# Outputs turned by transposes and chosen on DVE, values of four batches in one visit, tables made within the first tile: a perceiver layer on one core

## The reference, cut to what matters

```python
# stage 1: queries (128, 32, 128), context (128, 257, 128), mask (32, 257)
q, k, v = (a.reshape(B, n, 16, 8) for a in (layernorm(x), ctx, ctx))
A = softmax(einsum('blhe,bshe->bhls', q, k) / sqrt(8)) * mask
x = x + einsum('bhls,bshd->blhd', A, v).reshape(B, 32, 128)
# stage 2: x = x + attention(layernorm(x)) with a decay table in the lag of two tokens, and biases bq, bk, bv, bo
# stage 3: x = x + experts(layernorm(x)), with first-layer bias b1
```

## Time and profile before

| | us |
|---|---|
| median of 3 runs | 1048.88 (1048.84 to 1049.33) |
| profiled execution | 1050.45 |
| its span, first to last instruction | 1048.70 |
| first exponential of stage 1 | 23.97 |
| end of stage 1 (last addition to X) | 529.0 |
| busy: PE, DVE, ACT, POOL | 927.9, 840.0, 648.9, 606.9 |

### The profile page before, as it was taken

One profiled execution on the slowest core, in us unless ns is written; L12 is line 12 of the kernel. 1 busy time (PEld: TensorE's weight loads), 2 busy tenths in 40 slices (PEclk: granted clock), 3 DMA queues, 4 the chain that ended last, 5 costly groups with the idle time before them and its releaser, 6 DMA issues. The chain is left out here.

```text
span 1048.7 us, 25999 instructions
## 1 busy us (share of the span) xinstructions
PE 927.9 (88%) x7666; PEld 815.4 (78%) x7666; DVE 840.0 (80%) x2152; ACT 648.9 (62%) x2006; POOL 606.9 (58%) x531
## 2 busy tenths in 40 slices
PE   3959999999999999999948888878899888888983
PEld 2848888888888888888848888778788787878872
DVE  5747787878788787878758887886499999999995
ACT  2626566656666566666536666666477777767674
POOL 4335555655555564556344444443477777877786
PEclk9979999999999999999969998999999999999997
DMA  4021212212221212221400000000000000000000
GB/s 119 25 74 56 58 50 65 55 47 60 55 65 43 65 55 52 56 65 54 142 1 1 0 0 0 0 0 1 1 2 10 5 10 5 10 5 6 9 5 16
DMA packets 48676, 35.34 MB, mean 34 GB/s; under 512 B 3660, under 2 KB 48392, under 8 KB 48648
## 3 DMA queue, kind: packets, MB, share of 16 engines
q1 hardware_dynamic: 48648, 35.00, 12.2%
HBM read 32.88 MB, written 2.10 MB: 33 GB/s over the span
## 5 line engine op out<-in xcount | busy, mean ns | idle before, releaser
L551 ACT ACTIVATE E<-SC,neg_max 128x257 f32<-128x257 f32 x512 | 238.4, 471 | 161.2 <-DVE neg_max L613 161.1
L425 PE MATMUL SC<-Kt,Qbd 128*128 128x257 f32 x1024 | 279.6, 396 | 1.0 <-ACT E L551 0.8
L613 DVE TENSOR_REDUCE neg_max<-SC 128x2 f32<-128x514 f32 x256 | 177.0, 691 | 86.6 <-PE SC L425 75.2
L425 PEld LDWEIGHTS SC<-Kt,Qbd 128*128 128x128 f32 x1024 | 176.9, 193 | 31.4 <-issue 14.1
L301 POOL TENSOR_TENSOR Qbd<-Qt,head_scaled 128x2048 f32<-128x2048 f32 (+2 forms) x33 | 145.1, 4398 | 80.0 <-ACT Qt L541 80.0
L621 DVE TENSOR_TENSOR Et<-ETP,mask_T 128x512 f32<-128x512 f32 x256 | 174.0, 680 | 15.0 <-PE ETP L439 14.9
L439 PE MATMUL ETP<-ident,E 128*128 128x128 f32 x1024 | 156.1, 275 | 0.0
L1371 PE MATMUL PO<-W,hid 128*128 128x128 f32 x1024 | 138.2, 278 | 18.8 <-ACT hid L1412 18.7
L1371 PEld LDWEIGHTS PO<-W,hid 128*128 128x128 f32 x1024 | 131.4, 192 | 29.0 <-issue 21.5
L1436 ACT ACTIVATE Y<-Z,zb,zs 128x128 f32<-128x128 f32 x256 | 111.0, 485 | 60.1 <-DVE zb L1591 60.1
L439 PEld LDWEIGHTS ETP<-ident,E 128*128 128x128 f32 x1024 | 125.3, 142 | 20.5 <-issue 0.4
(11 more groups left out here) (161 smaller groups left out, 1579.1 us busy)
## 6 DMA issues: line engine op xcount, KB each, us to landing
V<-in_ctx_dram SPq DMA_DIRECT2D x64, 256.0 KB, 2.9
last_all<-in_ctx_dram SPq DMA_DIRECT2D x32, 256.0 KB, 5.0
xh<-in_x_dram SPq DMA_DIRECT2D x32, 64.0 KB, 3.7
X<-in_x_dram SPq DMA_DIRECT2D x32, 64.0 KB
out_dram<-Xo SPq DMA_DIRECT2D x64, 32.0 KB, 1.5
W<-in_L_ffn_w_dram SPq DMA_DIRECT2D x1, 1024.0 KB
W<-in_L_ffn_w_dram SPq DMA_DIRECT2D x2, 512.0 KB
last_row<-in_ctx_dram SPq DMA_DIRECT2D x32, 2.0 KB
```

The source lines that it names most:

```text
L425: i = pe.matmul(SC[s % 2][:, u, 0:S], Qbd[:, h, jj, g:g + HQ, :].rearrange("p q l -> p (q l)"), Kt[:, h, jj, 0:S], start=True, stop=True)
L551: i = act.activation(E[:, h, u0 + u, :], SC[s % 2][:, u, 0:S], ACT.Exp, bias=neg_max[:, s % 2, u:u + 1], accum_out=den[:, h, u0 + u:u0 + u ...
L613: dve.tensor_reduce(neg_max[:, s % 2, :], SC[s % 2][:, :, 0:S], AX.X, ALU.max, negate=True).then_inc(max_sb, 1)
```

## The change

- `turn_out` is four full transposes of O_m (128x128 each) into all 512 columns of MISC, in place of the products with `gather_d`, which is gone. O_m is no longer DVE's masked product but a plain copy of AV by ACT (`keep_sums`, behind the exponentials of step AV_STEP = 4, and of step 12).
- DVE chooses instead: a table `own_p` (`spread_shares`, at step 3, behind the reciprocal) holds the inverse sum where the head is the row's own and 0 elsewhere; `own_outputs` multiplies all 512 columns with it into own_x, `last_probs` makes last_p from it, four times as wide.
- POOL multiplies the last row's values with last_p in one operation (this one now gives o_last), and `fold` adds own_x, then adds heads in pairs twice, into O_n: two operations of 128x512, one of 128x256, one of 128x128 per half-tile, in place of one of 128x512, one of 128x256 and three of 128x128.
- `weigh_values` is called for four batches at once, at steps 2 and 10, for the half-tile before. Et holds 16 steps in place of 8. V of batches 0 to 3 is loaded behind the visit at step 10, of batches 4 to 7 behind the one at step 2 of the next tile.
- The tables are split: the lag's steps come earlier on DVE, ACT and POOL, PE's part comes at the end of steps 3 and 5 of tile 0 (into AV), DVE's at the start of steps 4 and 6; Kbd and Vbd are cleared in tile 0. On SP the second x, V and last rows come ahead of the weights.

```diff
 # SP
                     if not fresh:
                         sp.wait_ge(av_ps, TB * t)
                         sp.nop(nofuse=True)
+                        load_ctx(sp, t, 2)
                         load_ctx(sp, t, 3)
...
-                    sp.wait_ge(av_ps, TB * t + 2)
-                    sp.nop(nofuse=True)
-                    load_ctx(sp, t + 1, 0)
...
                     sp.wait_ge(av_ps, TB * t + 4)
                     sp.nop(nofuse=True)
+                    load_ctx(sp, t + 1, 0)
                     load_ctx(sp, t + 1, 1)
...
-                    sp.wait_ge(av_ps, TB * t + 6)
-                    sp.nop(nofuse=True)
-                    load_ctx(sp, t + 1, 2)
```

```diff
+                    pool.wait_ge(p_last, m + 1)
...
-                                       block_of[:, :].unsqueeze(1).unsqueeze(3).to_broadcast([P, HB * NQ, HQ, DK]),
...
-                    pool.tensor_tensor(last_o[:, :, :], last_v[:, :, :],
-                                       last_p[:, :].unsqueeze(2).to_broadcast([P, HB * NQ, DK]), ALU.mult).then_inc(o_last, 1)
-
-                def add_last(t, h):
+                                       last_p[:, :, :].unsqueeze(3).to_broadcast([P, HB * NQ, HQ, DK]),
+                                       ALU.mult).then_inc(o_last, 1)
+
+                def fold(t, h):
...
+                    pool.tensor_tensor(last_x[:, :, :, :], last_x[:, :, :, :], own_x[:, :, :, :], ALU.add).then_inc(o_sum, 1)
+                    pool.wait_ge(o_sum, m + 1)
+                    pool.tensor_tensor(pair_x[:, :, :, :], last_x[:, :, 0:2, :], last_x[:, :, 2:4, :], ALU.add).then_inc(o_pair, 1)
+                    pool.wait_ge(o_pair, m + 1)
+                    if h == 0 and not (isinstance(t, int) and t == 0):
+                        pool.wait_ge(o_t, t)
+                    pool.tensor_tensor(O_n[:, :, n * h:n * (h + 1)].rearrange("p d u -> p u d"),
+                                       pair_x[:, :, 0, :], pair_x[:, :, 1, :], ALU.add).then_inc(o_both, 1)
```

```diff
                 power(0, 0)
-                power(0, 1)
-                pool.wait_ge(dve_set, 1)
-                place_queries(0, 0, 0, 1, q_first)
-                place_queries(0, 0, 1, HB)
-
                 pool.wait_ge(act_set2, 2)
                 pool.affine_select(out=lag_ln[:, :], in_=lag_ln[:, :], compare_op=ALU.is_ge, fill=MASKED, base=0,
                                    pattern=[[-1, L]], channel_multiplier=1).then_inc(pool_set2, 1)
-                pool.memset(Kbd[:, :, :, :], 0.0).then_inc(pool_set2, 1)
-                pool.memset(Vbd[:, :, :], 0.0).then_inc(pool_set2, 1)
-                pool.wait_ge(dve_set, 11)
+                pool.wait_ge(dve_set, 1)
+                place_queries(0, 0, 0, 1, q_first)
+                power(0, 1)
+                place_queries(0, 0, 1, HB)
+                pool.wait_ge(dve_set, 10)
```

```diff
-                        i = pe.matmul(MISC[:, 32 * j:32 * j + 32], O_m[:, j, :], gather_d[:, :, :].rearrange("p g d -> p (g d)"),
-                                      start=True, stop=True)
+                        i = pe.transpose(MISC[:, j * P:(j + 1) * P], O_m[:, j, :], ident[:, :])
...
-                    if s % 4 == 3 and not (fresh and s < HSTEPS - 1):
-                        tt, ss = back(t, s, 2 + 5)
-                        weigh_values(tt, ss // 2, first=fresh and s < HSTEPS)
-                        weigh_values(tt, ss // 2 + 1)
+                    if s % HSTEPS == 2 and not (fresh and s < HSTEPS):
+                        tt, ss = back(t, s, HSTEPS + 2)
+                        for j in range(HB):
+                            weigh_values(tt, ss // 2 + j, first=fresh)
                     if s % HSTEPS == 5 and not (fresh and s < HSTEPS):
                         tt, ss = back(t, s, HSTEPS)
                         turn_out(tt, ss // HSTEPS)
...
+                def tables(n):
+
+                    if n == 0:
+                        pe.wait_ge(dve_set2, 8)
+                        pe.wait_ge(w2_in, 16 * 8)
+                        pe.matmul(TAB_LAG, turn_l[:, :, :].rearrange("p q l -> p (q l)"), lag_p[:, :], start=True, stop=True)
+                        pe.transpose(TAB_B, brow[:, :], ident[0:3, 0:3])
+                        pe.wait_ge(b1_in, 16)
+                        pe.transpose(TAB_B1, b1_rows[:, :], ident[0:NE * FH, 0:NE * FH]).then_inc(pe_set2, 1)
+                    else:
+                        pe.wait_ge(dve_set2, 11)
+                        pe.matmul(TAB_OUT, bcol[:, 2:3].to_broadcast([P, P]), W["o"][:, :], start=True, stop=False)
+                        pe.matmul(TAB_OUT, ones_row[:, :], bo_row[:, :], start=False, stop=True).then_inc(pe_set2, 1)
```

```diff
+                        if fresh and s in (3, 5):
+                            tables(s // 2 - 1)
+                        if fresh and s == 6:
+                            pe.wait_ge(dve_set2, 12)
...
-                pe.wait_ge(dve_set, 11)
+                pe.wait_ge(dve_set, 10)
...
                 run_tiles(steps, pe)
...
+                def keep_sums(t, h):
+
+                    m = 2 * t + h
+                    act.wait_ge(av_ps, HB * (m + 1))
+                    if not (isinstance(t, int) and t == 0 and h == 0):
+                        act.wait_ge(o_ps, m)
+                    act.activation(O_m[:, :, :], AV[:, :, :], ACT.Copy).then_inc(o_m, 1)
...
+                        if s % HSTEPS == AV_STEP and not (fresh and s < HSTEPS):
+                            keep_sums(*((t, 0) if s > HSTEPS else (t - 1, 1)))
```

```diff
+                def spread_shares(t, h):
+                    m = 2 * t + h
+                    dve.wait_ge(rden_set, m + 1)
+                    dve.tensor_tensor(own_p[:, :, :], rden[:, :].unsqueeze(2).to_broadcast([P, HB * NQ, HQ]),
+                                      block_of[:, :].unsqueeze(1).to_broadcast([P, HB * NQ, HQ]), ALU.mult).then_inc(own_set, 1)
...
+                        dve.wait_ge(o_sum, m)
+                    dve.scalar_tensor_tensor(last_p[:, :, :], E[:, h, :, S - 1].unsqueeze(2).to_broadcast([P, HB * NQ, HQ]),
+                                             mask_col[:, 0:1], own_p[:, :, :], ALU.mult, ALU.mult).then_inc(p_last, 1)
...
-                                      rden[:, :].unsqueeze(2).to_broadcast([P, HB * NQ, DK]), ALU.mult).then_inc(o_n, 1)
+                    dve.wait_ge(own_set, m + 1)
+                    if not (isinstance(t, int) and t == 0 and h == 0):
+                        dve.wait_ge(o_sum, m)
+                    dve.tensor_tensor(own_x[:, :, :, :], MISC[:, :].rearrange("p (u q d) -> p u q d", q=HQ, d=DK),
+                                      own_p[:, :, :].unsqueeze(3).to_broadcast([P, HB * NQ, HQ, DK]), ALU.mult).then_inc(o_n, 1)
```

```diff
+                        if fresh and s in (4, 6):
+                            tables(s // 2 - 2)
...
+                dve.wait_ge(pool_set2, 1)
+                dve.tensor_copy(lag[:, :], lag_i[:, :]).then_inc(dve_set2, 1)
                 norm_stats(0, 0)
+                dve.wait_ge(dve_set2, 1)
+                dve.tensor_scalar(lag[:, :], lag[:, :], 1.0, None, ALU.max).then_inc(dve_set2, 1)
...
+                for q in range(HQ):
+                    dve.tensor_copy(turn_l[:, q, :].rearrange("p (e r g) -> p e r g", e=2, r=HQ),
+                                    ident[0:L, 0:L].rearrange("p (g r e) -> p e r g", r=HQ, e=2)).then_inc(dve_set2, 1)
+                dve.tensor_copy(hh_wide[:, :, :], hh_of[:, :].unsqueeze(2).to_broadcast([P, HQ, TB])).then_inc(dve_set2, 1)
+                dve.wait_ge(pool_set3, 2)
+                dve.tensor_copy(iota_f[:, :], iota_i[:, :]).then_inc(dve_set3, 1)
+                dve.wait_ge(pool_set2, 4)
+                dve.tensor_copy(lag_p[:, :].rearrange("p (e r g) -> p e r g", e=2, r=HQ),
+                                lag_ln[:, :].rearrange("p (g r e) -> p e r g", r=HQ, e=2)).then_inc(dve_set2, 1)
                 place_last(0, 0)
                 norm_stats(0, 1)
                 norm_mean(0, 1)
                 norm_var(0, 1)
                 normalise(0, 1)
```

More of the change, by code:

```diff
@@ L30 @@
 HSTEPS = STEPS // 2
+AV_STEP = 4
 DECAY = -0.25
@@ L136, in perceiver_layer @@
             rden = sb1("rden", [P, HB * NQ])
-            Et = sb1("Et", [P, HSTEPS, 2, KT, HQ * L])
+            own_p = sb1("own_p", [P, HB * NQ, HQ])
+            Et = sb1("Et", [P, STEPS, 2, KT, HQ * L])
             O_m = sb1("O_m", [P, HB, HQ * L])
@@ L158, in perceiver_layer @@
             et_ps, et_sb = sem1("et_ps"), sem1("et_sb")
-            p_last, v_last, o_last, o_both = sem1("p_last"), sem1("v_last"), sem1("o_last"), sem1("o_both")
+            p_last, o_last, o_sum, o_pair, o_both = (sem1(n) for n in ("p_last", "o_last", "o_sum", "o_pair", "o_both"))
             q_first = sem1("q_first")
             av_ps = sem1("av_ps")
-            rden_set = sem1("rden_set")
+            rden_set, own_set = sem1("rden_set"), sem1("own_set")
             o_m, o_ps, o_n, o_t, x1 = (sem1(n) for n in ("o_m", "o_ps", "o_n", "o_t", "x1"))
@@ L346, in steps @@
```

(15 more changed lines are left out.)

100 lines of the change are left out of this document (25 added, 75 removed).

## The result

The changed kernel takes 1083.16 us (four runs, 1082.49 to 1084.53) against 1049.08 before (1048.84 to 1049.33): ratio 1.0327, 95% interval 1.0309 to 1.0344. It is 34 us slower; forecast were 22.6, in a range up to 1084. Its profiled execution took 1082.94, with a span of 1081.2.

What follows compares the result with a forecast made beforehand. PE was taken to bound stage 1, with only 0.28 of 15.19 us a half-tile waiting. Half-tiles +34.8, start -9.7, tables +0.6, SP's queue -4.9 and end +1.8 gave +22.6, so 1071.5 us against the medians, range 1058 to 1084.

Steps and rivals of the forecast that it cites:

- The sign: Whole kernel: slower by over 0.2% at chance 0.68, faster 0.27, within it 0.05.
- The new waits: Stage 1 loop: PE waits about 1.0 us for ACT's O_m, scores 8 wait 0.4 for the keys' copy.
- Rival (1): Stage 1 loop: PE stays the bound, -0.79 us a half-tile, 1013.8 us in all; chance 0.10.
- rival (2): Stage 1 loop: waits only eat the saving, ACT's copy precedes exponential 4, half-tile stays 15.19; 1036.7 us; chance 0.17.
- The steady half-tile: Stage 1 loop: 16.3 us a half-tile, +1.2 each, 29 of them +34.8.
- the layout: Stage 1 half-tile timed from row distances: 16.3 us for the changed kernel, 15.1 for the one before.
- The start: Ahead of the first exponential: it moves from 23.97 to 14.2 us, -9.7, bounds -10.5 and -7.
- the tables: Tile 0: the tables' products on PE, less one value visit, cost +0.6 us (0 to 2).
- SP's queue: Tile 1's wait for xh: earlier residual, no V load between, faster landing (-1.85, -1.5, -1.5), together -4.9 us.
- The end: Behind stage 1's last probabilities: ACT's copy, transposes, own outputs and three POOL additions, +1.8 us, bounds +1 and +2.5.
- The reference: Whole kernel: the profiled execution before lay 1.57 us above the median, so 1073.1 became 1071.5.
- rival 3: Stage 1: PE's waiting and transposes lower the clock, one half-tile in four hit, +14 us, 1085; chance 0.06.

Runs made afterwards that it cites:

- av_step3: The changed kernel with AV_STEP 3 for 4, so ACT copies AV behind the exponentials of step 3: 1065.64 us.
- short_max: The changed kernel with DVE's maximum reading only the first 64 of each group's 257 columns: 1059.94 us.
- start_x: The kernel before with only the new start, plus SP issuing 24 of 32 residual loads earlier and the next tile's loads ahead of the last 8: 1028.34 us.
- both_parts: turn_av3 with SP's load order from start_x: 1023.49 us, ratio to before 0.9746.
- both_spare: both_parts with an unused 128x32 tile declared where gather_d stood, moving later tiles by 128 bytes: 1024.47 us.
- av_step5: The changed kernel with AV_STEP 5 for 4, so ACT copies AV behind the exponentials of step 5: 1154.05 us.
- turn_av3: The changed kernel with value visits of two batches put back and ACT's copy behind exponential 3 (AV_STEP 3): 1036.28 us.

## Why the prediction was right, and where it was short

- **The time** lies in the range, but 0.8 us under its end, and 34.1 us is half as much again as the 22.6 forecast. The range isn't the sum of its own bounds: all at their upper ends they give 46.4 - 7 + 2 - 2 + 2.5 = +41.9, or 1091. The result also holds 3.5 us behind stage 1 and 1.8 of the reference (both below), which the sum didn't foresee. So that 1083.16 fell inside is in part luck; that the kernel is slower, and by which waits, is not.
- **The sign and the mechanism** were right. The new waits are at the places and within 0.3 us of the times laid out, and the half-tile grew by 1.38 where 1.2 was forecast. Rival (1), PE as the bound, fell with PE's 320 of 350 us, and rival (2) with the half-tile. Its first condition, ACT's copy ahead of exponential 4, was tried as av_step3, and that alone gives 15.98, not 15.19.
- **The steady half-tile, mis-sized**: the 29 of the sum cost 37.4 us, not 34.8 (434.5 before, 89.42 to 523.93, and 471.9 after, 78.64 to 550.55), and the one ahead of the stalled one, which stands in no term of the sum, 1.1 more (15.32 and 16.44). The half-tiles of the loop take 16.5 and 16.7 in turn, for 16.1 and 16.4 laid out. In the one without O_t scores 8 come at 9.47 for 9.25 although the keys' copy ends at 9.14 as laid out; this is the place where PE's loop over tiles begins anew, but no run shows that this is why. In the one with O_t the queries wait 0.35 for the normalising, as laid out (0.4). The value visit takes 1.89 to the next scores for 1.82. That the layout is too stiff against DVE shows in short_max too (0.80 for 0.52).
- **The shares of the parts** weren't in the prediction, which laid the whole out at once. Shown now: the joined visit 0.82 to 1.0, the late copy 0.6, the transposes themselves -0.25.
- **The start**: -10.0 for -9.7. Tile 0, though, from the first exponential to the first reciprocal, grew from 20.6 to 22.8, where 0.6 for the tables was forecast: +1.6. One trace can't settle this stretch: start_x took 21.3 in it in one profile and 22.4 in the other, both_parts 21.1, and both_spare, the same but for an unused tile, 22.7. The kernels that make the tables there lie between 21.1 and 24.1 for 20.6 before, so what the tables cost of the +1.6 isn't shown.
- **SP's queue**: the wait for xh fell to 7.23 ("near 7"), but the interval around it by 4.13, not 4.9, and in part for other reasons. From the end of POOL's first product to the landing of xh 22.99 us became 20.48, 2.5 less. The residual starts 1.85 sooner as forecast (0.49 behind that product), xh is issued 0.48 behind the residual's last load for 1.53 (-1.05 for -1.5), but it lands 7.07 us after its issue and not 5.0 (6.55 before): the -1.5 for this had nothing to it, and the other 1.6 of the 4.13 comes from the half-tiles around the wait, whose parts had moved against it. That the term came near is luck in part.
- **The end**: +2.3 for +1.8 (5.08 us from the last reciprocal to the last addition before, 7.42 after).
- These together make the end of stage 1 29.0 us later, not 22.6.
- **Stages 2 and 3**, forecast at nothing, took 523.2 for 519.7 us. 1.7 of it is in the steps of stage 3 (one takes 18.28 in the five kernels with gather_d and 18.37 in the nine with transposes, and the third is longer by 0.3). The rest, 1.8, lies ahead of these steps; the five kernels with gather_d, which have the same text there, took from 220.8 to 225.1 us for that stretch, and the changed kernel 223.3, so it is no more than their own spread.
- **The reference**: I took off 1.57 us, since the profiled execution of before lay that far above its median. That of after lay 0.2 under its own. 6.4 + 3.5 + 1.8 = 11.7 is the distance from 1071.5 to 1083.16.
- **The clock** (rival 3) stayed at full speed with PE idle 0.98 us at a stretch and 1.4 in a half-tile, and fell when the one wait was 2.5 (217.84 to 220.76, less 0.43, in av_step5). The price in the prediction, 1.9 a half-tile hit, was taken between two different starts (72.50 is a landing, not a reciprocal); av_step5 shows 1.5 (18.0 to 19.5) and 1.7 (18.2 to 19.9). The prediction's "most visits were transposes" doesn't hold by time: of the 4.5 us of visits in a half-tile before, keys and queries had 1.26. That four transposes took the place of four products did nothing to the clock all the same: turn_av3 and both_parts ran stage 1's loop at 1.00. The Trainium skill (TensorE: Matmul & The Clock Gate, "Part 4: PE-mode transpose") says that transposes don't count as busy in the same way. No run here, in which they always stand among products, shows a cost from that.

## What to carry to other kernels

Where PE is busy in every microsecond, ask what its visits to other work are covering before they are put together: here the steps between them ran on a loop through three engines and two buffers that was 0.28 us longer for two steps than PE's own work, and a saving of 0.4 on PE became a cost of 0.8. A copy has its place in its engine's list: one step earlier was worth 0.6 us a half-tile, one step later cost 2.4 (0.9 of it by the clock), and the other engine made no difference. And a change that comes out slower can hold parts worth keeping: the start, the transposes and a new order of 32 loads gave 2.5% together.

## What the runs showed that was not expected

- With one wait of 2.5 us in a half-tile of 18 PE's granted clock fell to 0.91 in about every second half-tile, though the same wait stands in each, at a cost of 0.9 us on average (18.98 against 18.1); with a wait of 1.0 in 16.5 it stayed at 1.00.
- Stage 3 takes 0.09 us a step longer in the kernels with transposes, as much as one addition of 128x16 on DVE does in the median (330 to 417 ns). Its text and operands are the same, and shifting the tiles by 128 bytes doesn't bring it back; the cause stays open.
- The same kernel's tile 0 differed by 1.1 us between two profiles (start_x), so a difference of that size in one trace's start says nothing.
- SP needed 0.79 us for each of 16 residual loads in a row (12.57 in all) before, and 0.54 for each of 8 (4.30) in start_x.
